# One more wait in front of each row gather: the gathers of a graph layer on GpSimd stay at most 36 tiles ahead of TensorE's multiplications

## The chip, the cores and the metric

The kernel runs on one core of one Trainium2 chip. The metric is the device time of one execution in microseconds (us), as the median of several runs; lower is better.

## The reference

A layer of a graph network over 50,000 nodes and 25,000 edges, with 256 features, all in float32. The edges come sorted by their target `dst`; their sources `src` are random. Cut to what matters:

```
h     = max(layernorm(x), 0)                            # x: 50000 x 256
msg   = relu(h[src] + edge_attr)                        # 25000 x 256
p     = msg @ W_fc.T + b_fc                             # 25000 x 256
scores = p @ Q.T                                        # 4 heads
alpha = softmax of scores over the edges that share dst
pooled[n, h] = sum over edges of n: alpha[:, h] * p
gate  = softmax(mean of p over the edges of n @ Wg.T + bg)
out   = x + sigmoid(sum over h: gate[n, h] * pooled[n, h])
```

The kernel normalizes only the rows of x that it has gathered by `src`, so that layernorm is computed once for each edge.

## The kernel before

The program has three parts, one after the other in the main.

**First part, edges.** The edges are cut into 196 tiles of 128 (`TILES`), the last of 40. A tile t goes through this row of steps, each on an engine of its own queue, with semaphores between them:

- GpSimd (POOL, "Pool" below) gathers the 128 rows `x[src]` of the tile by an indirect DMA (L314). For t below `RING` = 124 the rows go to their own place in `p_keep`, where the tile's result will later stand; from 124 on they go to one of 16 places (`BODY`) in `xg`, a part of `arena`. The semaphore `gathered[t % 16]` counts the landed gathers.
- VectorE (DVE) takes the statistics of the rows (`measure`, L727), and for four tiles together the mean and variance (`collect`, L755), the reciprocal of ScalarE's square root (`invert`, L760), and the negative mean times it (L762).
- ScalarE (ACT) takes the square root for four tiles (`root`, L381) and normalizes with relu (`normalize`, L366), which counts `ln_done`.
- DVE adds the edge attributes (`add_edge`, L733, counts `added`). SyncE (SP) loads these for four tiles at once into 16 places of `ea`, each when the earlier tiles there have been added.
- TensorE (PE) transposes the sum (`turn`, L545, two instructions, counts `turned`), ACT applies relu on the way out of PSUM (`relu`, L374, counts `relu_done`), PE multiplies by the weights (`multiply`, L555, four instructions, counts `multiplied`), and DVE adds the bias and takes the product out of PSUM (`evict`, L748 and L749, counts `p_out`).

The order on each engine is written out as one loop over k. DVE does `measure(k+7)`, `add_edge(k-1)`, `evict(k-6)`; ACT does `normalize(k)`, `relu(k-3)`; PE does `turn(k-2)`, `multiply(k-4)`. The buffers between them (`u`, `msg_t`, the PSUM banks) hold three or four tiles. From tile 132 on an eviction reuses one of eight places, whose content SP first writes to DRAM (`spill`, L249; 16 quads).

Pool's queue in this part holds nothing but the 196 gathers. Before the change, gather t waits for

- `gathered[t % 16]`, that is for the landing of gather t-16,
- once, at t = 90, for `tables_ready`, a set of tables that DVE has computed (until then scratch data lies in the places of `p_keep` from 90 on),
- and from t = 140 on for `ln_done` at t-15, that is for the normalization of tile t-16, whose place it takes.

So the first 140 gathers wait for no engine but the DMA's own, and the other 56 stay at most 16 tiles ahead of ACT.

**Second part, softmax over edges.** DVE scans over the logits of all tiles; it begins when all tiles are multiplied (first instruction L783).

**Third part, nodes.** PE adds up the rows by 586 small products (L613), ACT applies the sigmoid, Pool adds x, and the result is stored. It needs the second part's weights.

Of the kernel before, what the change touches and what calls it, by code (L numbers as in the profile page):

```python
# [35 lines left out]
def gnn_layer(nc, x, src, dst, edge_attr, w_fc, b_fc, q_w, g_w, b_g, out):  # L36
# [18 lines left out]
    STAGE = 8  # L55
    SPILL = TILES - RING - STAGE
    BEHIND = 12
    TURNS_IN = (0, 1, 6)
    assert RING % 4 == 0 and SPILL % STAGE == 0 and SPILL <= RING and TILES % 4 == 0

# [26 lines left out]
    with ExitStack() as ctx:  # L87
# [3 lines left out]
        def sem(name):  # L91
            return ctx.enter_context(nc.semaphore(name))
# [96 lines left out]
        multiplied, p_out, padded = sem("multiplied"), sem("p_out"), sem("padded")  # L189
# [13 lines left out]
        def rows_of(t):  # L203
            return LAST if t == TILES - 1 else P

        def x_row(t):
            return p_keep[0:rows_of(t), t, :] if t < RING else xg[0:rows_of(t), t % BODY, :]
# [7 lines left out]
        def _(sp):  # L215
# [20 lines left out]
            def load_ea(quad):  # L236
                if quad >= 4:
                    sp.wait_ge(added, 4 * quad - BODY + 4)
                to = ea[:, 4 * (quad % 4):4 * (quad % 4) + 4, :]
                if quad < QUADS - 1:  # L240
                    sp.dma_start(to, ea_rows[:, 4 * quad:4 * quad + 4, :]).then_inc(ea_in[quad % 4], 16)
                else:
                    sp.dma_start(to[:, 0:3, :], ea_rows[:, 4 * quad:4 * quad + 3, :]).then_inc(ea_in[quad % 4], 16)
                    sp.dma_start(to[0:LAST, 3, :], edge_attr[(TILES - 1) * P:E, :]).then_inc(ea_in[quad % 4], 16)

            def spill(n4):
                half = (n4 // 4) % 2
                sp.wait_ge(p_out, RING + n4 + 4)
                sp.dma_start(scratch[n4 // 4 * P:(n4 // 4 + 1) * P, :],  # L249
                             p_keep[:, RING + 4 * half:RING + 4 * half + 4, :].rearrange("p t d -> p (t d)")  # L250
                             ).then_inc(spilled[half], 16)

            for quad in range(QUADS):
                load_ea(quad)
                n4 = 4 * quad - RING - BEHIND
                if 0 <= n4 < SPILL:
                    spill(n4)
            for n4 in range(4 * QUADS - RING - BEHIND, SPILL, 4):
                spill(n4)
# [29 lines left out]
        @block.gpsimd  # L289
        def _(pool):  # L290
            pool.memset(src_i, 0).then_inc(pads_set, 1)
            pool.memset(dst_i, PAD).then_inc(pads_set, 1)
            pool.memset(ident[:, :], 0.0).then_inc(pool_step, 1)
            pool.wait_ge(pool_step, 1)
            pool.affine_select(out=ident[:, :], in_=ident[:, :], compare_op=ALU.not_equal, fill=1.0, base=0,
                               pattern=[[-1, P]], channel_multiplier=1).then_inc(const_set, 1)
            pool.memset(ones[:, :], 1.0).then_inc(const_set, 1)
            pool.iota(count_i, pattern=[[1, STEPS]], base=0, channel_multiplier=0).then_inc(const_set, 1)
            pool.iota(tile_i[:, :], pattern=[[P, BLK]], base=0, channel_multiplier=1).then_inc(const_set, 1)
            pool.memset(eps[:, :], LN_EPS).then_inc(const_set, 1)  # L300
            pool.memset(zero[:, :], 0.0).then_inc(const_set, 1)
            pool.memset(path[0:1, HALVES - 1, :], GROUPS).then_inc(const_set, 1)
            pool.memset(logits[:, TILES - 1:TP, :], 0.0).then_inc(const_set, 1)
            pool.wait_ge(idx_ready, 1)

            for t in range(TILES):
                k = t % BODY
                if t == RING - 34:
                    pool.wait_ge(tables_ready, 1)
                if t >= BODY:  # L310
                    pool.wait_ge(gathered[k], 16 * (t // BODY))
                if t >= RING + BODY:
                    pool.wait_ge(ln_done, t - BODY + 1)
                pool.indirect_dma_start(out=x_row(t), out_offset=None, in_=x,  # L314
                                        in_offset=bass.IndirectOffsetOnAxis(ap=idx[0:rows_of(t), t:t + 1], axis=0),
                                        ).then_inc(gathered[k], 16)

            x_later = x[0:FULL * GROUP * P, :].rearrange("(t p) d -> p t d", p=P)

            def add_four(g0, first, more):  # L320
                for slot in range(4):
                    pool.wait_ge(sig_done, g0 + slot + 1)
                    if first or slot not in BY_POOL:
                        pool.wait_ge(x_in[slot], g0 * 4 + 16)
                    else:
                        pool.wait_ge(x_pool[slot], g0 * 4)
                    pool.tensor_tensor(yout[:, slot, :, :], yout[:, slot, :, :], xin[:, slot, :, :],  # L327
                                       ALU.add).then_inc(summed, 1)
                    if slot in more:
                        pool.wait_ge(summed, g0 + slot + 1)  # L330
                        pool.dma_start(xin[:, slot, :, :], x_later[:, bass.ds((g0 + slot + XS) * GROUP, GROUP), :]  # L331
                                       ).then_inc(x_pool[slot], 16)

            add_four(0, True, BY_POOL)
            with pool.Fori(1, FULL // 4 - 1) as four:
                add_four(four * 4, False, BY_POOL)
            add_four(FULL - FULL % 4 - 4, False, [k for k in BY_POOL if FULL - FULL % 4 + k < FULL])
            for g in range(FULL - FULL % 4, GROUPS):
                slot = g % 4
                pool.wait_ge(sig_done, g + (2 if g == FULL else 1))  # L340
                if g < FULL and slot in BY_POOL:
                    pool.wait_ge(x_pool[slot], 16 * (g // 4))
                elif g == FULL and slot in BY_POOL:
                    pool.wait_ge(x_in[slot], 48)
                else:
                    pool.wait_ge(x_in[slot], 16 * (g // 4) + 16 + (16 if g == FULL else 0))
                whole = GROUP if g < FULL else (N - g * GROUP * P) // P
                ins = pool.tensor_tensor(yout[:, slot, 0:whole, :], yout[:, slot, 0:whole, :],
                                         xin[:, slot, 0:whole, :], ALU.add)
                if g == FULL:  # L350
                    left = N % P
                    ins.then_inc(pool_step, 1)
                    pool.wait_ge(pool_step, 2)
                    ins = pool.tensor_tensor(yout[0:left, slot, whole, :], yout[0:left, slot, whole, :],
                                             xin[0:left, slot, whole, :], ALU.add)
                ins.then_inc(summed, 1)
# [3 lines left out]
        def _(act):  # L360
# [8 lines left out]
            def relu(t):  # L369
                n = rows_of(t)  # L370
                act.wait_ge(turned, t + 1)
                if t >= 4:
                    act.wait_ge(multiplied, t - 4 + 1)
                nc.scalar.activation(msg_t[:, t % 4, :, 0:n],  # L374
                                     bank[:, TURNS_IN[t % len(TURNS_IN)], 0:D].rearrange("p (c e) -> p c e", c=KD)[:, :, 0:n],
                                     ACT.Relu).then_inc(relu_done, 1)
# [118 lines left out]
        def _(pe):  # L495
# [43 lines left out]
            def turn(t):  # L539
                n = rows_of(t)  # L540
                pe.wait_ge(added, t + 1)
                if t >= len(TURNS_IN):
                    pe.wait_ge(relu_done, t - len(TURNS_IN) + 1)
                for c in range(KD):
                    last = nc.tensor.transpose(bank[:, TURNS_IN[t % len(TURNS_IN)], c * P:c * P + n],  # L545
                                               u[0:n, t % 4, c * P:(c + 1) * P], ident[0:n, 0:n])
# [409 lines left out]
```

## Time and profile before

| | |
|---|---|
| median of 3 runs | 880.24 us (876.46 to 882.37) |
| the profiled execution | 881.09 us |
| its span in the profile | 879.3 us |
| busy: PE / DVE / ACT / Pool | 558.0 / 528.9 / 378.0 / 437.8 us |
| first part of the program | 0 to 449.24 us |
| second and third part | 449.24 to 879.3 us |

The profiled execution is taken as one of the same kind as the timed runs: it lies 0.85 us above their median. The 1.79 us between its time and its span lie outside of what the profile shows. Busy time is summed over the whole span; each part of the program has a limit of its own.

### The profile page before, as it was taken

The numbers are of one execution on the slowest core, as the hardware profiler recorded it, in microseconds if no ns is written. First come the engines' busy times: TensorE is split into PE (matmuls) and PEld (weight loads), VectorE is DVE, ScalarE is ACT, GpSimd is POOL, SyncE is SP. The second block draws the span as 40 slices with busy tenths as digits, with TensorE's granted clock in tenths as the row PEclk, the third lists the DMA queues.
The fourth block names the chain that finished last, engine by engine and source line by source line (L and its number), as shares of the span: only waits on it lengthen the run. The fifth ranks groups of instructions, "written<-read, shape, count | busy, mean of one in ns | idle before, by whom it ended". The sixth has DMA issues, their size and how long they took to land.

```text
span 879.3 us, 12486 instructions
## 1 busy us (share of the span) xinstructions
PE 558.0 (63%) x2436; PEld 425.6 (48%) x2437; DVE 528.9 (60%) x1878; ACT 378.0 (43%) x645; POOL 437.8 (50%) x334
## 2 busy tenths in 40 slices
PE   4104211117999999688950006988887888877885
PEld 3002101105877776566730005867776666656664
DVE  3621010015999999777988895756665555555553
ACT  0011000004777776455720020445665666576564
POOL 5777777730000004565200000557777778787887
PEclk9655555556999999999985556999999999999998
DMA  6334434311333434877600004999999999999998
GB/s 177 103 106 127 130 104 129 105 50 53 117 111 106 120 98 125 261 242 240 224 27 0 0 0 148 302 386 322 305 323 339 311 304 336 336 333 327 339 333 299
DMA packets 135059, 171.41 MB, mean 195 GB/s; under 512 B 8110, under 2 KB 121604, under 8 KB 135022
## 3 DMA queue, kind: packets, MB, share of 16 engines
q10 hardware_dynamic: 90496, 89.83, 31.3%
q1 hardware_dynamic: 31678, 42.99, 15.7%
q0 software_dynamic: 12848, 38.20, 13.9%
q8 instruction: 12, 0.20, 0.1%
q14 instruction: 25, 0.20, 0.1%
HBM read 111.39 MB, written 59.59 MB: 194 GB/s over the span
## 4 chain that ended last, share of the span: by engine, by line
PE 40%; another core or an unknown queue 19%; DVE 12%; issue 11%; ACT 7%; POOL 4%; ACTq 3%; DVEq 2%; DMA 2%; POOLq 0%
PE bank L555 19%; PE bank L613 14%; PE bank L545 6%; ACT arena L429 4%; POOL arena L327 3%; DVE spread L913 3%; ACT bank L402 2%; DMA arena<-in_x_dram 2%; DVE arena L867 2%; ACTq L432 1%; DVEq L917 1%; DVE arena L827 1%; DVE arena L822 1%; DVEq L913 1%
## 5 line engine op out<-in xcount | busy, mean ns | idle before, releaser
L327 POOL TENSOR_TENSOR arena<-arena 128x1024 f32<-128x1024 f32 x96 | 224.8, 2350 | 185.7 <-ACT arena L429 184.8
L613 PE MATMUL bank<-p_keep,spread 128*128 x1172 | 278.0, 392 | 57.9 <-DVE spread L913 47.8
L555 PE MATMUL bank<-w_all,arena 128*128 128x264 f32 (+1 forms) x784 | 226.7, 415 | 104.4 <-issue 81.3
L913 DVE TENSOR_SCALAR spread<-bank,rel,wgt 128x128 f32<-128x128 f32 x586 | 195.8, 404 | 136.5 <-PE bank L613 84.8
L613 PEld LDWEIGHTS bank<-p_keep,spread 128*128 128x128 f32 x1172 | 222.0, 194 | 113.7 <-issue 84.8
L555 PEld LDWEIGHTS bank<-w_all,arena 128*128 128x128 f32 (+1 forms) x784 | 143.5, 204 | 127.2 <-issue 86.3
L314 POOL DMA_INDIRECT arena<-in_x_dram,idx x72 | 69.3, 962 | 190.8 <-ACT arena L366 170.2
L429 ACT ACTIVATE arena<-bank 128x1024 f32<-128x1024 f32 x97 | 99.2, 1022 | 150.2 <-PE bank L613 133.7
L374 ACT ACTIVATE arena<-bank 128x256 f32<-128x256 f32 x196 | 72.6, 371 | 169.6 <-remote 108.6
L314 POOL DMA_INDIRECT p_keep<-in_x_dram,idx x124 | 118.4, 955 | 43.0 <-issue 37.5
L545 PE MATMUL bank<-ident,arena 128*128 128x128 f32 x392 | 83.5, 297 | 62.3 <-remote 46.7
L748 DVE TENSOR_TENSOR logits<-bank,bias 128x8 f32<-128x8 f32 x196 | 31.4, 160 | 132.8 <-remote 97.3
L545 PEld LDWEIGHTS bank<-ident,arena 128*128 128x128 f32 x392 | 50.8, 149 | 107.8 <-issue 56.7
L402 ACT ACTIVATE bank<-zero 128x1024 f32<-128x1024 f32 x98 | 100.5, 1026 | 3.0
L366 ACT ACTIVATE arena<-p_keep,negmr,rstd 128x256 f32<-128x256 f32 x124 | 73.0, 590 | 23.9 <-DVE negmr L762 20.8
L749 DVE TENSOR_TENSOR p_keep<-bank,bias 128x256 f32<-128x256 f32 x196 | 81.3, 415 | 0.5 <-issue 0.5
L733 DVE TENSOR_TENSOR arena<-arena 128x256 f32<-128x256 f32 x196 | 80.1, 408 | 1.3 <-issue 1.2
L727 DVE BATCH_NORM_STATS2 stats<-p_keep 128x6 f32<-128x256 f32 x124 | 50.7, 412 | 1.6 <-issue 1.0
L366 ACT ACTIVATE arena<-arena,negmr,rstd 128x256 f32<-128x256 f32 x72 | 42.7, 592 | 2.1 <-DVE negmr L762 1.5
L727 DVE BATCH_NORM_STATS2 stats<-arena 128x6 f32<-128x256 f32 x72 | 29.7, 413 | 0.0
L381 ACT ACTIVATE rstd<-mv,eps 128x4 f32<-128x4 f32 x49 | 14.5, 295 | 34.3 <-DVE mv L755 20.3
L331 POOL DMA_DIRECT2D arena<-in_x_dram x24 | 18.5, 770 | 17.6 <-POOL arena L327 14.8
(161 smaller groups left out, 184.5 us busy)
## 6 DMA issues: line engine op xcount, KB each, us to landing
out_dram<-arena ACTq DMA_DIRECT2D x97, 512.0 KB, 4.4
arena<-in_x_dram ACTq DMA_DIRECT2D x73, 512.0 KB, 5.3
arena<-in_edge_attr_dram SPq DMA_DIRECT2D x48, 512.0 KB
arena<-in_x_dram POOLq DMA_DIRECT2D x24, 512.0 KB, 5.7
p_spill<-p_keep SPq DMA_DIRECT2D x16, 512.0 KB
p_keep<-p_spill SPq DMA_DIRECT2D x16, 512.0 KB, 5.3
p_keep<-in_x_dram,idx POOLq DMA_INDIRECT x124
arena<-in_x_dram,idx POOLq DMA_INDIRECT x72
```

Of the source, the lines that this page charges most:

```text
L314: pool.indirect_dma_start(out=x_row(t), out_offset=None, in_=x, in_offset=bass.IndirectOffsetOnAxis(ap=idx[0:rows_of(t), t:t + 1], axis=0) ...
L327: pool.tensor_tensor(yout[:, slot, :, :], yout[:, slot, :, :], xin[:, slot, :, :], ALU.add).then_inc(summed, 1)
L366: nc.scalar.activation(u[0:n, t % 4, :], x_row(t), ACT.Relu, bias=negmr[0:n, m:m + 1], scale=rstd[0:n, m:m + 1]).then_inc(ln_done, 1)
L402: nc.scalar.activation(bank[:, 2 * z:2 * z + 2, :], zero[:, 0:1].unsqueeze(2).broadcast_to([P, 2, 512]), ACT.Copy).then_inc(zeroed, 1)
L429: nc.scalar.activation(yout[:, k % YS, :, :], places(k % SLOTS, GROUP), ACT.Sigmoid).then_inc(sig_done, 1)
L545: last = nc.tensor.transpose(bank[:, TURNS_IN[t % len(TURNS_IN)], c * P:c * P + n], u[0:n, t % 4, c * P:(c + 1) * P], ident[0:n, 0:n])
L555: last = nc.tensor.matmul(bank[0:n, 2 + t % 4, 0:NT], msg_t[:, t % 4, c, 0:n], w_all[:, c, :], start=(c == 0), stop=(c == KD - 1))
L613: nc.tensor.matmul(places[:, bass.ds(place, T)], spread[:, k0 + k, :], p_rows[:, bass.ds(p_at, T)], start=False, stop=True, skip_group_che ...
L727: v.bn_stats(stats[0:n, m, :], x_row(t)).then_inc(stats_done, 1)
L733: v.tensor_tensor(u[0:n, t % 4, :], u[0:n, t % 4, :], ea[0:n, t % BODY, :], ALU.add).then_inc(added, 1)
L749: v.tensor_tensor(to[0:n], bank[0:n, 2 + t % 4, 0:T], bias[0:n, 0:T], ALU.add).then_inc(p_out, 1)
L913: v.tensor_scalar(spread[:, k, :], bank[:, 7, P:2 * P], rel[:, bass.ds(s0 + k, 1)], wgt[:, bass.ds(s0 + k, 1)], ALU.is_equal, ALU.mult).th ...
```

## The change

Each gather from t = 36 on waits also until `multiplied` has reached t-35, that is until PE has multiplied tile t-36. Pool's queue holds the same 196 gathers in the same order; on the other engines nothing is changed. The instruction carries the new wait beside the one on `gathered`. From t = 140 on the wait on `ln_done` is there as before.

```diff
     BEHIND = 12
+    AHEAD_OF_PE = 36
     TURNS_IN = (0, 1, 6)
...
                 if t >= BODY:
                     pool.wait_ge(gathered[k], 16 * (t // BODY))
+                if t >= AHEAD_OF_PE:
+                    pool.wait_ge(multiplied, t - AHEAD_OF_PE + 1)
                 if t >= RING + BODY:
                     pool.wait_ge(ln_done, t - BODY + 1)
                 pool.indirect_dma_start(out=x_row(t), out_offset=None, in_=x,
```

## Rows read from the trace of the kernel before

**Rows 1.** Stretches of the first part: busy us (and instructions) by engine, clock, DMA share, GB/s

```profile
98.00:190.00 92.00, 15.58 (x36) 9.60 (x36) 6.41 (x27) 5.59 (x14) 65.80 (x70) 0.50 0.38 112
190.00:202.00 12.00, 0.00 (x0) 0.00 (x0) 1.41 (x6) 0.00 (x0) 0.00 (x0) 0.50 0.00 0
206.00:337.00 131.00, 130.65 (x647) 97.56 (x647) 129.13 (x596) 95.19 (x246) 0.00 (x0) 0.97 0.38 109
350.00:424.00 74.00, 59.54 (x275) 45.33 (x274) 56.48 (x253) 39.51 (x102) 44.76 (x47) 0.93 0.76 244
```

**Rows 2.** Waits from 100 to 190 us: total us, times, longest

```profile
DVE logits L748 <- remote: 76.6, 5, 15.7
ACT arena L374 <- remote: 76.5, 5, 16.0
...
POOL p_keep L314 <- issue: 15.8, 52, 0.3
```

**Rows 3.** Timeline of PE and ACT: the turn of tile 7, its relu, the next

```profile
96.35 0.69 PE L545 MATMUL bank<-ident,arena 128*128 128x128 f32 x2 [2.46 <-issue]
...
135.67 0.38 ACT L374 ACTIVATE arena<-bank 128x256 f32<-128x256 f32 x1 [15.83 <-remote]
136.11 2.13 PE L555 MATMUL bank<-w_all,arena 128*128 128x264 f32 x4 [14.33 <-issue]
...
152.53 0.38 ACT L374 ACTIVATE arena<-bank 128x256 f32<-128x256 f32 x1 [15.99 <-remote]
```

**Rows 4.** Timeline of Pool: gathers 0, 35, 36, 139, 140, 150 and 195

```profile
8.94 1.18 POOL L314 DMA_INDIRECT p_keep<-in_x_dram,idx  x1 [5.51 <-DVE idx L645]
...
53.61 0.94 POOL L314 DMA_INDIRECT p_keep<-in_x_dram,idx  x1 [0.30 <-issue]
54.86 0.95 POOL L314 DMA_INDIRECT p_keep<-in_x_dram,idx  x1 [0.30 <-issue]
...
183.88 0.95 POOL L314 DMA_INDIRECT arena<-in_x_dram,idx  x1 [0.30 <-issue]
337.68 1.14 POOL L314 DMA_INDIRECT arena<-in_x_dram,idx  x1 [152.86 <-ACT arena L366]
...
351.88 0.94 POOL L314 DMA_INDIRECT arena<-in_x_dram,idx  x1 [0.31 <-issue]
...
424.00 0.93 POOL L314 DMA_INDIRECT arena<-in_x_dram,idx  x1 [0.30 <-issue]
```

**Rows 5.** Stretches behind the last of the 140 gathers, and the first relu without delay

```profile
184.00:186.00 2.00, 0.00 (x0) 0.00 (x0) 0.00 (x0) 0.00 (x0) 0.82 (x1) 0.50 0.42 117
186.00:188.00 2.00, 1.33 (x3) 1.12 (x4) 0.00 (x0) 1.06 (x3) 0.00 (x0) 0.50 0.04 14
188.00:190.00 2.00, 1.23 (x4) 0.51 (x3) 0.00 (x0) 0.00 (x0) 0.00 (x0) 0.50 0.00 0
...
205.92 0.38 ACT L374 ACTIVATE arena<-bank 128x256 f32<-128x256 f32 x1 [2.71 <-PE bank L545]
```

**Rows 6.** Timeline of DVE and PE, the first tiles

```profile
56.62 0.18 DVE L760 RECIPROCAL rstd<-rstd 128x4 f32<-128x4 f32 x1 [4.13 <-issue]
59.20 0.66 PE L545 MATMUL bank<-ident,arena 128*128 128x128 f32 x2 [34.88 <-remote]
64.00 0.16 DVE L762 SCALAR_TENSOR_TENSOR negmr<-mv,rstd 128x4 f32<-128x4 f32 x1 [7.21 <-remote]
...
69.39 1.97 PE L555 MATMUL bank<-w_all,arena 128*128 128x264 f32 x4
...
91.93 1.97 PE L555 MATMUL bank<-w_all,arena 128*128 128x264 f32 x4
```

**Rows 7.** Waits from 350 to 424 us

```profile
POOL arena L314 <- ACT arena L366: 16.6, 15, 3.2
ACT arena L374 <- remote: 16.5, 6, 4.3
ACT arena L374 <- PE bank L545: 13.7, 9, 3.9
```

**Rows 8.** Timeline of DVE: the second part's first instruction

```profile
449.24 0.27 DVE L783 MEMSET arena<- 128x256 f32 x1
```

## Prediction

> **What bounds the kernel now.** I read the page's slices first. They show PE, DVE and ACT almost idle for a quarter of the span while Pool is busy, then the reverse. So the first part of the program was read by stretches, then by waits and line by line.
>
> The stretches [rows 1] show three regimes. From 98 to 190 us Pool issues 70 gathers, and PE executes 36 instructions. A tile costs PE six (two for the turn, four for the product), so that is six tiles in 92 us, or 15 us a tile and more. From 206 to 337 us Pool issues nothing, and PE and DVE are busy for 130.65 and 129.13 of 131 us: 647 / 6 = 108 tiles, 1.21 us a tile. From 350 to 424 us both go together.
>
> The first regime is the strange one. No data are missing: the gathers are more than 100 tiles ahead. The waits there [rows 2] say that ACT's relu and DVE's eviction each stand still for nearly 16 us a tile, "remote", so for nothing that the profile can name. The timeline names it [rows 3]. The turn of tile 7 ends at 96.35 + 0.69 = 97.04 us. Its relu starts at 135.67 us, 38.6 us later, though ACT is idle for the last 15.83 us of that and relu's other condition, an early product, was met long before. The reverse direction is prompt: that relu ends at 136.05 and PE's product starts at 136.11. So what comes late is the news of PE's finished work, as ACT and DVE see it, and PE's own wait of 14.33 us is only the echo. DVE shows the same with itself: the reciprocal at 56.62 us ends at 56.80, and the next instruction, which needs only that, starts at 64.00 [rows 6].
>
> The state goes with the gathers. They are issued from 8.94 to 183.88 us, 140 of them, one each 174.94 / 139 = 1.26 us with a gap of 0.30 us and no pause [rows 4]. Data stop moving by 188 us, the gathers are over then, nothing else runs, and still the delay goes on; at 205.92 us it is gone at a stroke [rows 5]. This reads like a backlog that back-to-back gathers pile up, and that takes 205.9 - 184.8 = 21 us to drain: (205.9 - 8.9) / 140 = 1.41 us for each gather issued at 1.26. What the backlog is made of, the trace does not say. What it costs is plain: twelve tiles are done at 206 us, where 1.21 us a tile would have needed 15 us.
>
> The third regime tells what gathers cost when they have to pause. There gather t waits for ACT's tile t-16. Pool stands still 15 times, at most for 3.2 us [rows 7], and ACT's waits for PE stay at most 4.3 us, not 16. Gathers 140 to 195 are issued from 337.68 to 424.00 us, 55 steps of 1.57 us [rows 4]. The first eleven of them, before SP's spills begin at 350.7 us, take (351.88 - 337.68) / 11 = 1.29 us each, the other 44 take 72.12 / 44 = 1.64 us, with the DMA share at 0.76 [rows 1].
>
> **The change part by part.** It adds 160 waits and removes nothing. The wait as such I put at nothing: from t = 140 on a gather has two conditions already, and the gap between gathers is 0.30 or 0.31 us there as before [rows 4]. Behind it on Pool's queue stand only later gathers, and who needs them is DVE's `measure`, 7 tiles ahead of the loop; PE's product is 4 behind. A gather is thus needed 11 tiles before its product, and 36 allows 25 tiles more, some 30 us at 1.21. No engine should wait for data.
>
> *Up to gather 35* nothing changes; it is issued at 53.61 us [rows 4]. Then Pool waits for tile 0's product, which lay at 69.39 us [rows 6]. The backlog drains meanwhile. By the rate above it is 36 x 0.15 = 5.4 us at 54.6 us, so gone near 60 us. The chain to the first product is the one of rows 6: DVE's 7.2 us wait ends early, near 60, then add, turn and product follow in some 2 us. I take 62 us for the first product, bounded by 59 (nothing is left of the delays) and 71.4 (as before, 69.39 + 1.97).
>
> *Gathers 36 to 139* then follow PE's products one by one: 104 gathers at a pace p. The trace has no row for this stretch of tiles with gathers beside them. The lower bound is Pool's own 1.26 us; the upper is 1.64, with spills, which this stretch does not have. Without spills the row is 1.29, but short, and begins with an empty backlog; the mean with spills is 1.57. I take p = 1.4, between them and equal to the drain rate of 1.41: 145.6 us. It ends at 207.6 us.
>
> *At gather 140* the old condition takes over, which is tighter. PE has then multiplied 104 tiles and ACT normalized about 109, while the gather needs tile 124 normalized. So Pool pauses for 15 tiles at the undisturbed 1.21 us: 18.2 us, to 225.8.
>
> *Gathers 140 to 195* run as before, 86.3 us, and from the last gather to DVE's second part it is 449.24 - 424.00 = 25.2 us as before [rows 4, 8]. The first part ends at 337.3 us in place of 449.24.
>
> *The rest* hangs only on that end and keeps its 879.3 - 449.24 = 430.1 us. The span becomes 767.4 us, and with the 1.79 us outside of it 769 us: 112 us less than the profiled 881.09. Against the median of 880.24 it is the same within a microsecond. What is late next is DVE and PE at 1.21 us a tile and, beside gathers, the shorter delays of the third regime.
>
> In one formula the time is 769 + 104 x (p - 1.4) + (first product - 62).
>
> **The rivals.** *The pace of the third regime holds throughout*, since its delays come from gathers beside tiles and not from spills: p = 1.57 to 1.64 gives 787 to 794 us, with a late first product (71.4) up to 803. For it speaks that ACT's waits of up to 4.3 us start after only five gathers; against it, the 1.29 us. A gate fed by PE's late news, where ACT's is prompt [rows 3], may let the delay swing more: p = 1.9 gives 821.
>
> *Pool's own pace*: if pauses are so frequent that no backlog forms, p = 1.26 gives 754, and 736 if the catching up at gather 140 disappears as well because tiles go ahead early.
>
> *The gathers are not the cause*, and the bad state simply lasts to 206 us whatever Pool does. This is the case that ends slower. Then at 206 us 12 tiles are done and only 48 gathers, where 140 were. The other 92 of this stretch have to run beside the tiles at 1.57 instead of not at all: 206 + 92 x 1.57 + 18.2 + 86.3 + 25.2 = 480 us, 31 us later than 449, so 912 us. The head start of Pool is what is given away. Against it stands that the third regime shows the same waits, in small, as soon as gathers come back.
> The Trainium skill speaks for this rival ("DMA: Bandwidth & Descriptors", section on the anatomy of one DMA on the gpsimd path): a DMA issued by GpSimd costs about 2.0 us plus its bytes at 436 GB/s, which makes an estimate of 2.3 us for 128 KB, its semaphore update some 100 ns, and many descriptors can be given out before their extra cost shows. By that rule the gathers ahead are harmless. The trace agrees with the landing, over within about 3 us after the last issue, but not with an end of the trouble there, which comes 18 us later.
>
> *The throttled gathers still hold PE's news*, one after the other, and Pool and PE drag each other. From the first product to the fifth the trace has (91.93 - 69.39) / 4 = 5.6 us a tile [rows 6]. The gain is lost when p passes 1.4 + 112 / 104 = 2.48; at 5.6 it would be 1206 us. Against it: Pool can't issue back to back for long when PE is that slow, and each pause drains the backlog.
>
> *The change does nothing*, because PE is always far enough: excluded as long as the first product comes after 54.86 us, where gather 36 was issued before.
>
> **How the numbers follow.** My forecast, 750 to 780 us, has 0.45; the third regime's pace, 780 to 821, 0.31; below 750, 0.08; a worse swing, 821 to 870, 0.07; within 1% of the time before, 0.02; slower, 0.07, of which 0.05 for the cause lying elsewhere and 0.02 for the dragging. The range of 735 to 820 us holds a little over 8 in 10. One per cent is about what a measurement of this kernel can tell from no change. Faster 0.91, same 0.02, slower 0.07.
>
> **What the profile after would show.** Pool's gathers stop after the 36th near 54.6 us and resume with the first product; were that after 75 us, my start is wrong. "Remote" waits of 16 us are gone, and the longest of ACT's relu is below 5 us. Tile 124 is normalized near 225 us, with Pool idle before gather 140 for under 20 us in place of 152.86. PE's granted clock, 0.50 from 98 to 190 us, is near the 0.93 of the third regime [rows 1], which matters since at the low clock a product takes 1.97 us; if PE's gaps kept it low, p would pass 2. Second and third part together stay at 430 us. The forecast fails if the stall outlives the pause at 54.6 us, or if p is far from 1.4.

## The result: 785 us, and the profile after

| | median | ratio to before |
|---|---|---|
| before, 4 runs | 878.35 us (876.19 to 882.37) | |
| changed, 4 runs | 784.74 us (780.76 to 786.46) | 0.892, 95% interval 0.887 to 0.898 |

The profiled execution took 786.46 us with a span of 784.8 us. The forecast was 769 us in a range of 735 to 820.

The page's busy tenths in 40 slices: PE in the kernel before, then PE and its granted clock in the changed kernel. PE now fills the slices 4 to 9, where it was busy for one to four tenths:

```profile
PE   4104211117999999688950006988887888877885
...
PE   5208887788889877793000499898878787787785
PEclk9658999999999998997555599999999999999998
```

The stretches of 22 us (columns as in [rows 1]):

```profile
66.00:88.00 22.00, 18.79 (x94) 13.55 (x92) 17.37 (x81) 11.68 (x31) 14.48 (x15) 1.00 0.62 181
...
198.00:220.00 22.00, 17.13 (x85) 12.49 (x85) 17.63 (x82) 13.02 (x35) 13.98 (x14) 1.00 0.54 176
220.00:242.00 22.00, 21.42 (x110) 16.06 (x109) 21.14 (x96) 15.64 (x41) 4.72 (x5) 1.00 0.43 126
```

In each stretch of 22 us from 66 to 220 us, PE executes 84 to 94 instructions beside 14 or 15 gathers; before, it executed 36 in 92 us [rows 1]. The stretch from 220 us has only 5 gathers, and there PE gets 110 done.

Pool's timeline, gathers 35 and 36, then 139 and 140, then the last (those of before are [rows 4]):

```profile
53.34 0.95 POOL L317 DMA_INDIRECT p_keep<-in_x_dram,idx  x1 [0.30 <-issue]
63.72 0.95 POOL L317 DMA_INDIRECT p_keep<-in_x_dram,idx  x1 [9.43 <-PE bank L558]
...
224.09 0.95 POOL L317 DMA_INDIRECT arena<-in_x_dram,idx  x1 [0.30 <-issue]
241.39 1.12 POOL L317 DMA_INDIRECT arena<-in_x_dram,idx  x1 [16.35 <-ACT arena L369]
...
329.29 0.93 POOL L317 DMA_INDIRECT arena<-in_x_dram,idx  x1 [0.30 <-issue]
```

The first product and, much later, DVE's first instruction of the second part, which was at 449.24 us [rows 8]:

```profile
60.95 1.97 PE L558 MATMUL bank<-w_all,arena 128*128 128x264 f32 x4
...
356.47 0.27 DVE L786 MEMSET arena<- 128x256 f32 x1
```

The waits from 64 to 224 us (total us, times, longest). The 16 us waits of [rows 2] are gone; what is left looks like [rows 7]:

```profile
POOL p_keep L317 <- PE bank L558: 38.7, 27, 9.4
ACT arena L377 <- remote: 33.8, 18, 3.9
ACT arena L377 <- PE bank L548: 25.2, 20, 3.0
...
DVE logits L751 <- remote: 17.3, 11, 2.3
```

The first part of the program is 92.8 us shorter (449.24 to 356.47), the other two together went from 430.1 to 784.8 - 356.5 = 428.3 us.

### The profile page after: what moved, and what is told of

Read it like the earlier page. It is cut to its first block, busy times and chain, and to the rows that moved or that the text cites. A ratio compares the mean times of both kernels' runs of the same rounds, so it can differ in the third digit from the quotient of the medians.

```text
span 784.8 us, 12589 instructions
## 1 busy us (share of the span) xinstructions
PE 551.3 (70%) x2436; PEld 420.7 (54%) x2437; DVE 531.2 (68%) x1878; ACT 378.6 (48%) x645; POOL 443.1 (56%) x334
## 3 DMA queue, kind: packets, MB, share of 16 engines
q0 software_dynamic: 12848, 38.20, 15.0%
## 4 chain that ended last, share of the span: by engine, by line
PE 38%; DVE 23%; issue 10%; ACT 9%; another core or an unknown queue 7%; POOL 5%; ACTq 4%; DVEq 2%; DMA 1%; SPq 1%; POOLq 0%
PE bank L616 17%; PE bank L558 14%; POOL arena L330 4%; PE bank L548 4%; ACT arena L432 4%; DVE spread L916 3%; DVE p_keep L752 3%; DVE stats L730 2%; DVE arena L736 2%; ACT bank L405 2%; DVE arena L870 2%; ACTq L435 2%; ACT arena L369 2%; DVEq L920 1%
## 5 line engine op out<-in xcount | busy, mean ns | idle before, releaser
L558 PE MATMUL bank<-w_all,arena 128*128 128x264 f32 (+1 forms) x784 | 220.4, 406 | 47.5 <-ACT arena L377 30.7
L558 PEld LDWEIGHTS bank<-w_all,arena 128*128 128x128 f32 (+1 forms) x784 | 138.6, 197 | 72.2 <-ACT arena L377 37.8
L317 POOL DMA_INDIRECT p_keep<-in_x_dram,idx x124 | 122.6, 989 | 74.7 <-PE bank L558 38.7
L548 PE MATMUL bank<-ident,arena 128*128 128x128 f32 x392 | 80.6, 289 | 33.4 <-remote 33.1
L334 POOL DMA_DIRECT2D arena<-in_x_dram x24 | 18.5, 771 | 17.6 <-POOL arena L330 14.8
L528 PE MATMUL bank<-arena 128*128 128x512 f32 (+1 forms) x8 | 4.2, 691 | 32.2 <-DVEq L908 32.2
```

The lines of the kernel that those rows point to most:

```text
L558: last = nc.tensor.matmul(bank[0:n, 2 + t % 4, 0:NT], msg_t[:, t % 4, c, 0:n], w_all[:, c, :], start=(c == 0), stop=(c == KD - 1))
```

## The experiments

The twelve experiments ran in four jobs, each on one chip with its own runs of the kernel before. The kernel before took 875.39 us in the first job (7 runs), 706.90 in the second (7 runs), 707.57 in the third (13 runs) and 875.24 in the fourth (7 runs), on four different chips. Within a job its runs never differed by more than 1.3%, experiment 11 included. So there are chips on which the kernel before is slow and chips on which it is not, and each result below says which it met. I call them chips of the 875 and of the 707 kind. No chip was met in two jobs, so whatever else came with a job is not told apart from its chip. Which kind the first run of this study met is plain from its 878.

### On chips of the 875 kind

**1. A pause without a gate.** The wait on PE is left out; Pool executes a small memset of its own ahead of each gather.

```diff
+                pool.memset(filler[:, :], 0.0).then_inc(paced, 1)    # filler: 128 x 256
+                pool.wait_ge(paced, t + 1)
                 pool.indirect_dma_start(out=x_row(t), ...
```

> The kernel before (no wait on PE), but Pool executes one small memset of its own (128x256, on a tensor that nothing else uses) and waits for its end ahead of each gather, which stretches the step from gather to gather from 1.26 us to an estimated 1.6 to 1.8 us. Theory A (the delays come from gathers issued faster than some 1.4 to 1.56 us each, and the order or PE's progress do not matter): no waits near 16 us, twelve tiles are multiplied long before 200 us, and the time is 750 to 800 us although Pool never looks at PE. Rival B (what helps is that Pool is tied to PE's progress): the stall stays and the time is above 850 us.

Measured: 765.29 us, ratio 0.874 (0.870 to 0.879), against 875.39. Pool's timeline shows a step of about 1.55 us:

```profile
100.50 0.95 POOL L319 DMA_INDIRECT p_keep<-in_x_dram,idx  x1 [0.27 <-POOL filler L317]
101.44 0.33 POOL L317 MEMSET filler<- 128x256 f32 x1
102.05 1.09 POOL L319 DMA_INDIRECT p_keep<-in_x_dram,idx  x1 [0.27 <-POOL filler L317]
```

and the waits from 60 to 200 us name the landing of the gathers in the place of late news:

```profile
DVE stats L732 <- DMA p_keep<-in_x_dram,idx: 21.1, 17, 2.9
```

Theory A holds and B falls: 0.3 us more between gathers, and nothing else, takes away the stall. PE's progress need not be looked at. Where ACT was idle before a relu, it started at most 0.04 us after its turn had ended; in the kernel before that was up to 47.6 us, in the changed kernel still up to 5.6 us. The first product starts at 44.24 us, against 60.95 in the changed kernel.

The paced kernel even beats the change by some 2% (0.874 against 0.892). Its 196 gathers take from 9.1 to 317.8 us without a break, and the first part ends at 336.1 us. Of the 20.4 us less than in the changed kernel, about 11.5 come from the last gather, which leaves sooner, and about 9 from the tiles behind it, which are done sooner after it. The mean step over gathers 36 to 139 is no shorter than the changed kernel's (1.58 us against 1.557); what differs is how evenly they go. The gate lets several gathers go about 1.25 us apart and then stops Pool (51 of these 103 steps are below 1.3 us, the longest is 3.09), the pause sets every gather apart (none below 1.5).

**2. A gate on ACT's news.** `relu_done` in the place of `multiplied`:

```diff
-                    pool.wait_ge(multiplied, t - AHEAD_OF_PE + 1)
+                    pool.wait_ge(relu_done, t - AHEAD_OF_PE + 1)
```

> The changed kernel with the gate on relu_done, which ACT counts, in place of multiplied, which PE counts, same distance of 36. The trace shows ACT's news prompt and PE's late. Theory C (PE's late news makes Pool's bursts and pauses swing, and this is why a gather and a tile took 1.56 us and not 1.4): 1.40 to 1.48 us a gather, time 770 to 777 us. Rival D (1.56 is what a gather beside a tile costs, however it is gated): within 5 us of the changed kernel's 785.

Measured: 785.75 us, ratio 0.896 (0.892 to 0.901). Theory C falls and rival D holds: a prompt signal in the gate brings nothing. Gather 36 leaves earlier, at 55.00 us, but the delays then hold Pool up once for 5.3 us, and gather 139 leaves at 224.49 us against 224.09 in the changed kernel.

**3. A busy Pool without gathers.** For tiles 32 to 127 the rows are filled with a constant by memsets on Pool; 96 of 196 gathers are left out.

```diff
+                if 32 <= t < 128:
+                    pool.memset(filler[:, :], 0.0).then_inc(filled, 1)      # 128 x 512
+                    pool.wait_ge(filled, 2 * (t - 32) + 1)
+                    pool.memset(x_row(t), 0.5).then_inc(filled, 1)
+                    pool.wait_ge(filled, 2 * (t - 32) + 2)
+                    continue
```

> The kernel before, but for tiles 32 to 127 nothing is gathered: Pool fills the rows with a constant by memsets of about the same total duration, so it is as busy and as far ahead, without a DMA. Leaves out 96 of 196 gathers. Theory A (the DMAs of the gathers make the backlog): no 16 us waits after 50 us, tiles at 1.2 us, the first part ends near 305 us and the time is near 737 us. Rival E (a busy Pool by itself delays the others' signals): the stall stays until about 185 us and the time is above 850 us.

Measured, in a single run: 750.42 us. From 60 to 140 us Pool is busy for 70.35 of 80 us and PE without a gap:

```profile
60.00:140.00 80.00, 79.99 (x409) 60.86 (x408) 78.78 (x365) 58.54 (x150) 70.35 (x169) 0.99 0.36 108
```

409 / 6 = 68 tiles in 80 us, 1.17 us a tile. Rival E falls: it is the gathers, not Pool's being busy with instructions of its own. (The memsets took about 0.95 us a tile in all, against 1.26 for a gather's step.) The first part ended at 319.9 us where I expected 305, and the time is 13 us above my 737. The first 32 tiles are still gathered without a pause, and their delays stay: the first product starts at 56.96 us. The rest of that miss was not traced.

**4. Plain DMAs in the place of gathers.** Same rows by number and size, from Pool's queue, without the indices (the indexing is left out):

```diff
-                pool.indirect_dma_start(out=x_row(t), out_offset=None, in_=x, in_offset=...)
+                pool.dma_start(x_row(t), x[t * P:t * P + rows_of(t), :])
```

> The kernel before, but Pool's 196 gathers are plain DMAs of the same 128 rows x 1 KB from consecutive rows of x (leaves out the indexing). Issue gets shorter, an estimated 1.1 us a step. Theory F (any DMA that Pool issues back to back makes the backlog): the waits near 16 us stay or grow, time 860 us or more. Rival G (the indirection makes it): no such waits, and the time is below 790 us.

Measured, in a single run: 706.29 us. Rival G's outcome came. The DMAs leave every 0.54 us, more than twice as fast as gathers, and fill the DMA engines; PE and DVE run beside that as if nothing were there:

```profile
66.00:88.00 22.00, 21.99 (x114) 16.67 (x113) 21.86 (x103) 15.73 (x42) 17.47 (x34) 1.00 1.04 342
```

The longest wait of ACT's relu for PE up to 85 us is 1.1 us. The page counts 12848 packets and 38.20 MB on Pool's DMA queue in both this kernel and the kernel before. So neither the bytes nor the number of packets nor their rate makes the delay. The edit changed two things, though: the form of the DMA, and the rows, which are consecutive here and scattered over x in the gathers. Plain DMAs from scattered rows were not tried, so that it is the indirect form is argued and not shown. The time that the packets of Pool's queue took hardly depends on either: as a share of the span of 16 engines it is 13.9% of 879.3 = 122 us in the kernel before, 16.3% of 704.4 = 115 us here, and 17.2% of 707.4 = 122 us in experiment 9, with gathers on a chip of the 707 kind.

**12. The gate at 18 tiles** (`AHEAD_OF_PE = 18`), after experiment 8 with the same kernel.

> The gate at 18 tiles. Where the kernel before takes near 707 us: slower, 721 to 724, since Pool stands still for 13.6 us before the first product, gathers then run beside tiles at 1.26 us a step and none of that time comes back. Where it takes near 878 us: first product near 45 us, p = 1.56, no pause at gather 140, a time near 777 us, 8 us less than at 36.

Measured: 766.93 us, ratio 0.877 (0.871 to 0.882), against 875.24. Pool's timeline, gathers 17 and 18:

```profile
31.26 0.94 POOL L317 DMA_INDIRECT p_keep<-in_x_dram,idx  x1 [0.30 <-issue]
46.45 0.94 POOL L317 DMA_INDIRECT p_keep<-in_x_dram,idx  x1 [14.25 <-PE bank L558]
```

The first product comes near 46 us instead of 63, gather 139 leaves at 233.28 and gather 140 at 234.53 us, without the pause of 16.35. The step between is (233.28 - 46.45) / 121 = 1.54 us, as with 36 tiles. My sum for the first part came out 9 us too long, mostly in the last piece: from gather 195 to the second part it is 338.9 - 320.1 = 18.8 us, where I had taken 25.

**11. The kernel before, once more, for its trace.**

> The kernel before, for its trace. If it runs near 707 us: Pool's gathers 1.26 us apart up to the 140th as in the slow case, but ACT's relu follows PE's turn at once, no wait near 16 us, first part over near 275 us; the second and third part take the same 430 us as where it runs near 878. If it runs near 878 us: the trace of the first profile again.

It met the 875 kind and gave 881.16 us with the same waits (DVE's eviction "remote" 5 times, at most 15.6 us). The trace of the kernel before on a chip of the 707 kind was not taken.

### On chips of the 707 kind

**5 to 8.** The expectations of these four were written for the other kind, and that makes most of them void.

> As the paced run, with a memset of 128x16 ahead of each gather, an estimated 1.35 to 1.45 us from gather to gather in place of 1.55. Theory A1 (the backlog grows by the step short of 1.41 us a gather, as the drain behind the 140 gathers gave it): at 1.40 hardly any delay, and since 196 gathers then take some 275 us, the time is 735 to 750 us. Rival A2 (1.56, the step that the gated gathers took, is the true cost): backlog grows by 0.15 us a gather, stalls come back in part, and the time is above 770 us.

```diff
+                pool.memset(filler[:, :], 0.0).then_inc(paced, 1)    # filler: 128 x 16
+                pool.wait_ge(paced, t + 1)
```

Measured: 727.06 us, where the kernel before took 706.90: ratio 1.027 (1.024 to 1.029). The step is 1.35 us, with the longer ones 1.39 in the mean over gathers 36 to 139. DVE waits for landings 10 times from 60 to 200 us, at most 1.4 us. The question between A1 and A2 was not answered, since on this chip there is no delay to take away.

> As the paced run, with a memset of 128x512, an estimated 1.75 us from gather to gather. Both theories: no late news at all, DVE waits for landings, and the first part is as long as 196 gathers: 9 + 196 x 1.75 + 20 = 372 us, so a time near 800 us.

The same with a filler of 128 x 512. A single run: 809.37 us, first part 377.5 us, gathers from 9.4 to 360.3 us or 1.80 us a step. This is Pool's pace alone, and came about as expected. It is 14% slower than the kernel before on this chip.

> The changed kernel (gate of 36 tiles on multiplied) with the short memset of 128x16 ahead of each gather. Theory A1: the bursts at 1.26 us are what makes the delays of the changed kernel, so the short pause takes them away and the time is within 10 us of the short-paced run without the gate, 740 to 755. Rival H (the gate itself costs, by the pauses at its start and at gather 140): 765 to 785.

The short filler with the change's gate. Measured: 727.29 us, ratio 1.028 (1.026 to 1.030), the same as without the gate.

> The changed kernel with 18 in place of 36. If only the step p = 1.56 of gathers beside tiles counts, Pool pauses earlier, the first product comes earlier (near 45 us in place of 63) and no pause is left at gather 140: 45 + 122 x 1.56 + 88 + 25 = 348 us for the first part, a time near 777 us. If the reserve of 36 is needed, DVE waits for gathers and the time is above 790 us.

A single run: 722.85 us against 706.90, so 2.3% slower. Pool stands still before gather 18 for 13.64 us, and the first part is over at 293.7 us.

**9. The changed kernel.**

> The changed kernel itself, once more. In the last four runs the kernel before took 707 us on the chip that they ran on, where it had taken 875 to 880 on the chips of all other runs; no 16 us waits were seen there at gathers 1.26 us apart. Theory J (late news is a matter of the chip, not of the program alone). If the kernel before takes near 707 us here, the gate has next to nothing to hold: gather 36 comes at 54.9 us, the first product near 45 us, and a step of 1.26 us never catches up with tiles at 1.21, so the changed kernel is within 1% of it. If the kernel before takes near 878 us, the changed one repeats 785. Rival K (the 707 was an accident of that job, and the same chip gives either): the ratio varies within one chip.

Measured: 706.85 us (10 runs) against 707.57 (13 runs), ratio 0.998 (0.996 to 1.001). Here the change does nothing. Theory J holds as far as four jobs can tell: each chip kept its kind through all runs of its job, which speaks against K. The mean step over gathers 36 to 139 is 1.27 us here, against 1.557 with the same kernel on the other kind. The timeline at gathers 36 and 37 shows why the gate is idle; "PE" is named as the last condition, but the gap stays 0.30 or 0.31 us:

```profile
56.40 0.95 POOL L317 DMA_INDIRECT p_keep<-in_x_dram,idx  x1 [0.31 <-PE bank L558]
57.65 0.94 POOL L317 DMA_INDIRECT p_keep<-in_x_dram,idx  x1 [0.30 <-PE bank L558]
```

And PE's news is prompt with gathers going out back to back. The turn at 46.89 us ends at 47.53, the relu starts at 47.56:

```profile
46.89 0.64 PE L548 MATMUL bank<-ident,arena 128*128 128x128 f32 x2
...
47.56 0.38 ACT L377 ACTIVATE arena<-bank 128x256 f32<-128x256 f32 x1 [1.13 <-PE bank L548]
```

From 98 to 190 us, 73 gathers and 461 / 6 = 77 tiles go side by side, where the other kind of chip did 6 tiles in the kernel before [rows 1]:

```profile
98.00:190.00 92.00, 91.95 (x461) 66.94 (x460) 91.35 (x424) 65.50 (x171) 69.65 (x73) 1.00 0.71 213
```

The traces of the two kinds differ in one more thing. The page gives no time from issue to landing for gathers on the 875 kind (first line, the kernel before), and gives it here (second line):

```profile
p_keep<-in_x_dram,idx POOLq DMA_INDIRECT x124
...
p_keep<-in_x_dram,idx POOLq DMA_INDIRECT x124, 3.4
```

The reason lies in the records of semaphore increments. The 196 gathers make 196 x 16 = 3136 of them; the trace of experiment 9 holds 3111, that of experiment 4 all, and that of the kernel before 467. The changed kernel's holds 806 and the paced one's 1561. So on the 875 kind records are missing whenever gathers run, also in the paced kernel, where ACT sees the end of PE's turns within 0.04 us.

**10. The short pause again.**

> The kernel with the short memset of 128x16 ahead of each gather again, 1.35 us from gather to gather as its first run showed. Where the kernel before takes near 707 us: 727 again, since DVE waits for landings. Where it takes near 878 us: theory A1 (a gather costs some 1.41 us there) says a backlog of 0.06 us a gather, waits of a few us and 740 to 765 us; rival A2 (it costs 1.56) says stalls of 10 us and more for part of the time and above 790 us.

726.56 us, ratio 1.024 (1.019 to 1.030): once more the 707 kind. How far below 1.55 us the step may go on the 875 kind stays untried.

## Why the prediction was right, and where it was off

*What bounds the kernel*: the reading that PE's finished work becomes known late, and that gathers without a pause cause it, is shown by experiments 1 and 3 on the chips where it happens, and experiment 4 shows that plain DMAs of consecutive rows don't cause it. The rival with a cause that lasts to 206 us whatever Pool does is out.

The trace of before tells more than I read in it. It also records when semaphores rise, and it is the increment itself that is late, not its being seen. The turn of tile 7 ends at 97.04 us; `turned` rises at 135.64, and the relu starts 0.03 us after that. Around 206 us the held-up increments come about 0.1 us apart: `turned` rises at 205.89, 205.99 and 206.09 us, and `multiplied` at 205.85, 205.95 and 206.05.

Beside the rival that the gathers are not the cause I had set what the Trainium skill says ("DMA: Bandwidth & Descriptors", "Anatomy of one DMA — SWDGE (gpsimd) path"): many descriptors can be given out before their extra cost shows. That gathers ahead are therefore harmless to other engines was my own step, for the page speaks only of the DMA's cost. The step agrees with experiment 4 and with the 707 kind of chip; for gathers on the 875 kind it does not.

*The sum, term by term*, from the two fences of the timeline and [rows 4, 8]:

| term | forecast | measured |
|---|---|---|
| gather 36 leaves after the first product | 62 | 63.72 |
| gathers 36 to 139 | 104 x 1.40 = 145.6 | 103 steps of 1.557 = 160.4 |
| pause before gather 140 | 18.2 | 17.3 |
| gathers 140 to 195 | 86.3 | 87.9 |
| to the second part | 25.2 | 27.2 |
| end of the first part | 337.3 | 356.5 |
| second and third part | 430.1 | 428.3 |

Five of the terms are within 2 us. The one that was mis-sized is p, the step of a gather beside tiles: 1.56 us in place of 1.40, which is 14.8 of the 17.4 us by which the span missed. (The forecast's 104th step is the one to gather 140; in the measured column it is a part of the pause.) The total of 785 us lies in the range, but above the 750 to 780 us that I held most likely. The rival with the third regime's pace had it right, at 787 us.

Part of this miss is a wrong count. Gathers 140 to 150 are eleven gathers but ten steps, so without spills the row gave 14.20 / 10 = 1.42 us and not 1.29, and with them 72.12 / 45 = 1.60 and not 1.64. Rightly counted, the rows spoke for 1.42 to 1.60. That the forecast's 1.40 still lies close to the 1.42 is luck: it was taken between 1.29 and the longer rows, and from the drain rate. The changed kernel's stretch has no spills and takes 1.56 all the same. On the 707 kind the same kernel takes 1.27 (experiment 9), so the rest of the step is the delays that remain on the 875 kind and not a price of gathers beside tiles.

The prediction also says that in the first regime the gathers are more than 100 tiles ahead. At 98 us it is 71 gathers against 6 products, and 100 is reached only near 145 us. Nothing in the sum hangs on that.

*The late signal in the gate*, which I thought might make p swing to 1.9, did not matter (experiment 2). *PE's clock* recovered as said: granted 0.92 to 1.00 in every stretch from 66 to 352 us. Tile 124 was normalized near 240.6 us, where I had said 225, which is again the long step. *The wait itself* cost nothing: the gap between gathers stayed 0.30 us where the condition had been met.

*What I did not see*: that the disease is one of the chip it runs on. All numbers of the prediction came from chips of the 875 kind, and the result too. On the 707 kind the same change is worth 0.998. Nothing in the trace of before could tell this.

*What stays open*: what it is in a gather that delays PE's and DVE's news, and what differs between the chips. One rival stands untested. Every execution timed here has a span and a granted clock on record, so the profiler was recording in all of them; records of increments are missing, while gathers run, on just the kind of chip where increments come late, and whether the recording has a part in the delay, or in the difference between chips, no run tells. The drain rate gave 1.41 us a gather, the steps beside tiles 1.54 to 1.56; whether a step between 1.26 and 1.55 us would do on the 875 kind was tried twice and met the other kind both times.

## What to carry to other kernels

An engine that runs far ahead at no visible cost may still be what holds the others. When several engines wait 16 us for "remote" on work that was finished long before, look for who issues without a pause, and stretch its step before building a gate: a memset of 0.33 us did more here than a semaphore on PE. Then time the pair of kernels on more than one chip. The pause that gains 13% on the 875 kind (a step of 1.55 us) was not run on the 707 kind; there a step of 1.35 us cost 2 to 3% and one of 1.80 us 14%. By a straight line between these two, 1.55 us would take an estimated 764 us, 8% more than the kernel before. A gate far enough behind (36 tiles) gains 11% on the one and costs nothing on the other. No version was shown to be better than both kernels on both kinds of chip; on the 875 kind alone the paced one (765 us) and the gate at 18 tiles (767 us) were.

## What the runs showed of the hardware

- The same program takes 875 us on some Trainium2 chips and 707 on others, stable within a job (34 runs of the kernel before over four chips, each met in one job, with the profiler recording).
- On the first kind, gathers of 128 rows x 1 KB issued 1.26 us apart delay the semaphore increments of PE's and DVE's instructions, with up to 16 us of standing still a tile; 1.55 us apart, evenly, they don't. Plain DMAs of the same size from consecutive rows, 0.54 us apart at up to 342 GB/s, don't either.
- There most records of semaphore increments are missing from the trace while gathers run: 467 of 3136 are left for the gathers of the kernel before, and 3111 on the 707 kind (experiment 9).
- ACT's signals were not late in the same stretch: 0.06 us from its relu to PE's product [rows 3].
